# A merge table for five engines, made anew

## Time and profile before

| | |
|---|---|
| median of 3 runs | 3286.13 us (3277.07, 3286.13, 3286.29) |
| profiled execution, span | 3287.9 us |
| PE busy | 2907.9 us, 88% of the span |
| DVE busy | 2739.3 us, 83% |
| ACT busy | 2096.2 us, 64% |
| POOL busy | 1925.7 us, 59% |
| DMA | 308.56 MB, mean 94 GB/s |
| first scan of chunk 0, last scan of chunk 15 | 98.1 us, 3041.5 us |

### The profile page before, as it was taken

The page is one execution under the profiler, slowest core; times in us unless marked ns, Lnnn a source line. Parts: engine busy times, 40 slices in busy tenths (PEclk is TensorE's granted clock), DMA queues, the critical chain, the costliest instruction groups (busy, mean ns, idle before and its releaser), DMA issues.

```text
span 3287.9 us, 45422 instructions
## 1 busy us (share of the span) xinstructions
PE 2907.9 (88%) x14848; PEld 2380.8 (72%) x14848; DVE 2739.3 (83%) x4612; ACT 2096.2 (64%) x3852; POOL 1925.7 (59%) x1541
## 2 busy tenths in 40 slices
PE   6567698998999899898989989899999989998898
PEld 4455477787877778687777868777777877777676
DVE  3777989797998979799898979889897989989541
ACT  2546476676757677675767767576766767575433
POOL 1766667564766757475675756576575647666110
PEclk8558699999999999999999999999999999999998
DMA  4241123231322323232322323232232323223122
GB/s 130 96 159 39 52 81 111 92 102 64 129 82 91 125 78 100 70 118 85 100 103 81 106 79 125 66 106 92 87 109 86 108 76 121 78 71 120 56 103 76
DMA packets 152778, 308.56 MB, mean 94 GB/s; under 512 B 18368, under 2 KB 96984, under 8 KB 135136
## 3 DMA queue, kind: packets, MB, share of 16 engines
q1 hardware_dynamic: 152000, 302.52, 27.6%
q10 hardware_dynamic: 272, 1.57, 0.1%
q0 software_dynamic: 272, 1.57, 0.1%
HBM read 288.27 MB, written 17.35 MB: 93 GB/s over the span
## 4 chain that ended last, share of the span: by engine, by line
PE 48%; DVE 18%; issue 13%; ACT 12%; POOL 5%; DMA 1%; DVEq 0%; SPq 0%; POOLq 0%; ACTq 0%
PE ps_B L1870 11%; PE ps_B L1765 10%; PE ps_A L1765 8%; DVE hs L1527 8%; PE ps_H L1760 7%; DVE acc L1491 5%; PE ps_H L1778 4%; PE ps_B L1760 3%; POOL bu L1100 3%; PE ps_B L1778 3%; PE ps_B L1917 2%; ACT ps_A L1288 2%; DMA bb<-b_rows 1%; DVE hA L1719 1%; ACT acc L1300 1%
## 5 line engine op out<-in xcount | busy, mean ns | idle before, releaser
L1100 POOL TENSOR_TENSOR bu<-z,bb 128x512 f32<-128x512 f32 x1024 | 1294.2, 1290 | 289.9 <-DVE hs L1527 146.7
L1527 DVE TENSOR_TENSOR_SCAN hs<-ps_A,state,bu 128x512 f32<-128x512 f32 x768 | 976.5, 1276 | 21.7 <-ACT ps_A L1288 11.4
L1288 ACT ACTIVATE ps_A<-dt,a_neg 128x512 f32<-128x512 f32 x1024 | 699.3, 686 | 355.7 <-DVE hs L1527 351.5
L1760 PE MATMUL ps_H<-ident,hs 128*128 128x128 f32 x4096 | 652.6, 294 | 195.3 <-DVE acc L1491 123.1
L1760 PEld LDWEIGHTS ps_H<-ident,hs 128*128 128x128 f32 x4096 | 528.3, 151 | 329.2 <-DVE acc L1491 152.0
L1870 PE MATMUL ps_B<-ws_out,hid 128*128 128x256 f32 x2944 | 699.4, 382 | 15.5 <-ACT hid L1437 6.1
L1491 DVE SCALAR_TENSOR_TENSOR acc<-ps_H,ctok,acc 128x512 f32<-128x512 f32 x960 | 700.2, 731 | 8.0 <-PE ps_H L1760 7.1
L1870 PEld LDWEIGHTS ps_B<-ws_out,hid 128*128 128x128 f32 x2944 | 537.0, 191 | 85.1 <-ACT hid L1437 9.9
L1765 PE MATMUL ps_B<-fh,ws_in 128*128 128x512 f32 x1440 | 537.6, 418 | 10.3 <-DVE bl L1680 4.3
L1527 DVE TENSOR_TENSOR_SCAN hs<-ps_A,bu 128x512 f32<-128x512 f32 x256 | 310.9, 1216 | 32.2 <-ACT ps_A L1288 20.0
L1765 PEld LDWEIGHTS ps_B<-fh,ws_in 128*128 128x128 f32 x1440 | 271.0, 188 | 70.5 <-DVE cb L1664 8.1
(11 more groups left out here) (349 smaller groups left out, 4807.7 us busy)
## 6 DMA issues: line engine op xcount, KB each, us to landing
ws_in<-w_split SPq DMA_DIRECT2D x126, 1024.0 KB, 5.4
bb<-b_rows SPq DMA_DIRECT2D x256, 256.0 KB, 3.9
ws_out<-in_L_ffn_V_rwkv SPq DMA_DIRECT2D x64, 512.0 KB, 5.8
ws_out<-in_L_ffn_W SPq DMA_DIRECT2D x32, 512.0 KB, 6.9
xb<-in_L_attn_x SPq DMA_DIRECT2D x16, 512.0 KB, 5.3
n<-in_L_attn_x SPq DMA_DIRECT2D x16, 512.0 KB, 3.9
w_split<-wsp SPq DMA_DIRECT2D x8, 1024.0 KB, 5.6
out<-xb SPq DMA_DIRECT2D x16, 512.0 KB, 3.2
```

Of the source, the lines that this page charges most:

```text
L1100: pool.tensor_tensor(bu[:, u % 4, :], z[:, d, :], bb[:, s % 2, :], ALU.mult)\
L1288: act.activation(b.t[:, :], dt[:, d, :], ACT.Exp, scale=a_neg[:, d, s:s + 1])\
L1527: dve.tensor_tensor_scan(hs[:, s % 2, d, :], b.t[:, :], bu[:, k % 4, :], state[:, s, d:d + 1] if i % CPB else 0.0, ALU.mult, ALU.add)\
L1760: return pe.transpose(dst, src, ident[:, :])
```

## The change

Every number of the table PACE is set anew, on all five engines, for all four streams and for the last f and x. No piece, instruction, wait or buffer is other, and no line of code but the table. The table has four lines less, so that a line of the code has a number 4 lower after than before. Two of its lines on POOL, as they were and are:

```diff
-        "u1": 25, "u2": 25, "u3": 25, "xg": 39, "rstd_a": 106, "x_prob": 146, "end_rstd_a": 116, "end_x_prob":
...
+        "u3": 22, "xg": 36, "rstd_a": 106, "x_prob": 152, "end_rstd_a": 110, "end_x_prob": 121, "rstd_e": 169, "h2":
```

More of the change, by code:

```diff
@@ L168 @@
     "sp": {
[6 rows of a table removed]
-        253, "e1_1": 265, "e1_1_down": 267, "out": 286, "last_mod_x": -26, "last_rv": 161, "last_sw": 172,
-        "last_e0_0": 204, "last_e0_1": 209, "last_e0_0_down": 221, "last_e0_1_down": 232, "last_e1_0": 240,
-        "last_e1_0_down": 277, "last_e1_1": 346, "last_e1_1_down": 346, "last_out": 348,
[8 rows of a table added]
+        "last_out": 377,
     },
     "pool": {
[3 rows of a table removed]
-        152, "rstd_e": 164, "h2": 190, "x_bias": 191, "rstd_h": 214, "rstd_i": 219, "rstd_j": 220, "rstd_m":
-        238, "x5": 286, "last_rstd_e": 169, "last_h2": 170, "last_x_bias": 172, "last_rstd_h": 179,
-        "last_rstd_i": 181, "last_rstd_j": 186, "last_rstd_m": 192, "last_x5": 260,
+        "w_low0": 44, "w_low1": 47, "w_low2": 51, "w_low3": 59, "w_low4": 75, "w_low5": 88, "w_low6": 96, "w_low7":
+        112, "mean0": -53, "rstd0": -31, "h0": -27, "mean1": -14, "rstd1": -1, "gx": 13, "u0": 22, "u1": 22, "u2": 22,
+        "u3": 22, "xg": 36, "rstd_a": 106, "x_prob": 152, "end_rstd_a": 110, "end_x_prob": 121, "rstd_e": 169, "h2":
+        185, "x_bias": 193, "rstd_h": 211, "rstd_i": 211, "rstd_j": 212, "rstd_m": 238, "x5": 282, "last_rstd_e": 148,
+        "last_h2": 150, "last_x_bias": 150, "last_rstd_h": 150, "last_rstd_i": 161, "last_rstd_j": 162, "last_rstd_m":
+        162, "last_x5": 236,
     },
     "act": {
[21 rows of a table removed]
[20 rows of a table added]
     },
     "dve": {
[5 rows of a table removed]
-        201, "ao1": 204, "h_stats": 204, "h_norm": 206, "i_stats": 208, "i_norm": 208, "j_stats": 209, "lowx0":
[4 rows of a table removed]
-        164, "last_ao1": 165, "last_h_stats": 165, "last_h_norm": 165, "last_i_stats": 173, "last_i_norm": 173,
[4 rows of a table removed]
[14 rows of a table added]
     },
     "pe": {
[27 rows of a table removed]
[25 rows of a table added]
     },
```

## The result

The kernel with the new table takes 3341.8 us (median of 4 runs, 3326.9 to 3343.4) against 3285.0 for the kernel before: ratio 1.0162, with a 95% interval of 1.0144 to 1.0180. It is slower by some 55 us where I had said 15, and lies outside my range. The profiled execution has a span of 3341.4, 53.5 more than the one before.

The account below looks back on a forecast made before the run. DVE was taken to pace the stretches and PE the boundaries; terms summed to 1.3 us per chunk, by 14 = 18, less 3 for the ends = +15, giving 3301 us, range 3264 to 3318.

Parts of the forecast that it names:

- an edit can cost only where it makes PE or DVE stand still: Premise for the whole kernel: DVE paces the stretches, PE the boundaries; edits pay only where one of them stands idle.
- e_norm, +0.3 for each chunk: Chunk's end: scan 62 loses its 0.78 wait, but nE and PE's boundary run start up to 0.37 later; +0.3 us.
- Gates, +0.2: Boundary: gate 2 waits uncovered for gate 0's copy, so z0, softplus and the next stretch come later; +0.2 us per chunk.
- the clock had nothing to give back: Boundary: PE's granted clock reads 1.00, its upper level (2.4 GHz), so nothing can be got back from it.
- x_prob, +0.5, by a late bu 31: POOL: x_prob behind bu 30 delays bu 31, so DVE stands 0.5 us at scan 31 in each chunk.
- x2, +0.6: DVE behind unit 32: x2 meets POOL's bu, still catching up, and contends for SBUF operands; +0.6 us per chunk.
- The rest ... I cost them at nothing: Rest of the stretch: pieces moved by a few units, where bu and dA lead the scans by several us; 0.
- Transposes of unit 56, -0.3: PE: transposes of units 56 and 57 go ahead of p5 and p7, removing one of two DVE waits; -0.3 us per chunk.
- The ends, -3: Chunk 0 gains 1 us as POOL's store comes earlier; the tail gains 2 by hiding PE's wait and earlier statistics.
- a share against a full block: x2's price beside a bu: 0.47 us from the stretch alone, up to 1.25 if the shared port locks fully.

Follow-up runs that it names:

- x9: New table with x_prob, choice with sg, e_norm, gates and h1T at their former places, x2 behind unit 27: 3285.7 us, ratio 1.0000.
- x11: As x9, but with e_norm behind unit 62 as in the new table; gates and h1T as before: 3291.4 us, ratio 1.0015.
- x10: As x9, but with the boundary (e_norm, gates and h1T) as in the new table: 3296.2 us, ratio 1.0030.

## Why the prediction was wrong

The direction held, and so did the terms of e_norm, the gates, x2 and the transposes, in kind and nearly in size. Two steps failed: the term of x_prob, which put that move at +0.5 by a wait that did not come, where the move cost 1.43 in another place; and the step that cost the other moves at nothing, where choice alone cost 1.47. Behind both is the premise that an edit can cost only where it makes PE or DVE stand still: I looked for waits ahead of an instruction, and the loss was inside the instructions. By its own steps:

- *e_norm, +0.3 for each chunk:* 0.30 in chunk 8, 0.33 in the traces of x9 and x11, 0.41 by their medians. *Gates, +0.2:* 0.28 in the traces of x11 and x10, 0.34 by their medians. Both right, a little small. That the clock had nothing to give back was read from a window that begins where the lower level ends; it changed no term.
- *x_prob, +0.5, by a late bu 31:* this step failed. In the new table scan 31 waits for POOL in no chunk (in chunk 9 its bu ends 2.35 ahead), since DVE is late itself by then. That scan 31 starts 0.52 later in the mean is ACT's dA 31; the agreement with +0.5 is luck. The price of the move was at scan 22: 1.43 for each chunk, 20 us, and 24 in the kernel with x_prob back. I asked what hid x_prob and not what x_prob's own wait was hiding, the 5.24 of the earlier trace rows: it kept POOL still while DVE made the two fl. The same move in the old table costs 0.67 there; the rest of the 1.43 I put down to mean0's new place, which I had cost at nothing and which was not set back by itself.
- *x2, +0.6:* 0.54. Right, with its cause, and its cover in the old table was the wait of rstd0, as I said; that the place behind unit 36 is no better in the new table I had not seen.
- *"The rest ... I cost them at nothing":* this step failed too. Choice, moved behind unit 27, was not even named there; its last two operations meet the bu that start when the row of B lands. 1.47 for each chunk between the tables, 27 us in the trace of the kernel with choice back. I looked at each move for what waits for it; at what runs beside it on the other engine I looked for x2 alone. With 1.43 + 1.47, and with the 0.52 at scan 31 whatever its cause, the sum of the stretch and the boundary is 14 x (1.3 + 2.9) = 59, against 55.7 measured.
- *Transposes of unit 56, -0.3:* -0.48 in the traces, -0.3 (4 us by 14) by the kernel with this one thing.
- *The ends, -3:* chunk 0 became 1.3 longer and not shorter, chunk 1 1.6 longer, the first boundary 2.5 and the tail 3.4 shorter (2 said). That it is -2.2 in all is luck; how it divides was not tried.

For x2's price I weighed a share against a full block; the full block is what the Trainium skill's page "SBUF — State Buffer" (section "SBUF: two separate sides") states. The runs are for the block: wcs, 0.16 by itself, ended with the bu beside it after 1.04. That rule names every DVE operation with two operands in SBUF, and I applied it to one of them.

What stays open: how much of the loss at the two fl needs mean0's new place; why wcs came in between two bu, behind the first, and x2 in chunk 4 stood through four; why PE is late for the hid pair ahead of dA 31. The boundary's two parts, 10.5 us by x9 and x10, are 3.5 more than my terms for them, which is within the intervals.

## What to carry to other kernels

When a piece is moved on one engine, ask what its wait was keeping still: an engine that stands can be the cover of another one's work. Before moving anything, list the operations that are longer when the neighbour runs (here DVE's with two operands in SBUF, beside POOL's), and look in the new order for which of them a neighbour's operation falls on; a busy time that grows with the same instructions is how it shows in a profile. And a load that waits for a piece ties it to everything queued behind that load. Last, where a term comes out at the right size, see in the trace whether the engine that was to be late is the one that is waited for.

## What the runs showed of the hardware

Beside a POOL operation on SBUF, a DVE operation with two operands in SBUF stood until that operation ended, however small it was (0.17 became 1.04 and 1.20; two of 0.64 became 2.68 beside two bu). Where POOL had several queued it could stand through more than one: x2, 1.22 alone, took 5.84 beside four bu in a row in the kernel with choice back. POOL stood too: five bu took 6.65 with an fl between them, where 1.25 each would be 6.25. An operation of DVE with one operand in SBUF (a reciprocal of 0.18) or with one in PSUM (the scan, 1.27) had the same length beside bu as without.
